# Causal mask of a half of the scores: one VectorE operation over both PSUM banks instead of one for each bank

## What is computed

```python
def _decay_mask(L):
    n = jnp.arange(L)
    nm = n[:, None] - n[None, :]
    g = jnp.asarray(GAMMAS)
    return jnp.where((nm >= 0)[None], g[:, None, None] ** jnp.maximum(nm, 0)[None], 0.0)

def _msr(X, WQ, WK, WV, WG, WO, gnw, gnb, D):
    Q = _xpos(jnp.einsum('bsh,nhd->bnsd', X, WQ), False)
    K = _xpos(jnp.einsum('bsh,nhd->bnsd', X, WK), True)
    V = jnp.einsum('bsh,nhd->bnsd', X, WV)
    A = jnp.einsum('bnsd,bntd->bnst', Q, K) * D[None]
    Y = jnp.einsum('bnst,bntd->bnsd', A, V)
    ...
    return G * jax.nn.sigmoid(G) * Yn @ WO
```

## Time and profile before

| | us |
|---|---|
| median of 3 runs | 2426.39 (2426.34 to 2426.5) |
| the profiled execution | 2424.55 |
| its span, first to last instruction | 2422.7 |
| busy: PE, DVE, POOL, ACT | 2223.8, 1869.4, 1762.4, 1550.3 |
| mean granted TensorE clock | 0.984 of full |

### The profile page before, as it was taken

One profiled execution on the slowest core, in us unless ns is written; L12 is line 12 of the kernel. 1 busy time (PEld: TensorE's weight loads), 2 busy tenths in 40 slices (PEclk: granted clock), 3 DMA queues, 4 the chain that ended last, 5 costly groups with the idle time before them and its releaser, 6 DMA issues.

```text
span 2422.7 us, 52427 instructions
## 1 busy us (share of the span) xinstructions
PE 2223.8 (92%) x18306; PEld 1940.9 (80%) x18306; DVE 1869.4 (77%) x5586; ACT 1550.3 (64%) x4986; POOL 1762.4 (73%) x1758
## 2 busy tenths in 40 slices
PE   0389999999999999999999999999999999996984
PEld 0268888888888888888888888888888888886874
DVE  6457888878787888888888888787888887867543
ACT  0156776776767777677677776767777677763442
POOL 4786777777777777777777777777777774334777
PEclk9989999999999999999999999999999999998997
DMA  2813131312122222213131313122221111002875
GB/s 98 311 40 101 25 112 29 111 29 96 44 72 67 72 69 71 72 29 111 27 112 27 110 30 113 28 72 66 72 69 36 34 28 36 1 30 79 254 229 158
DMA packets 110527, 192.17 MB, mean 79 GB/s; under 512 B 24388, under 2 KB 44998, under 8 KB 110160
## 3 DMA queue, kind: packets, MB, share of 16 engines
q1 hardware_dynamic: 66640, 97.96, 11.6%
q0 software_dynamic: 33280, 67.45, 9.9%
q10 hardware_dynamic: 10368, 23.67, 3.3%
HBM read 100.30 MB, written 89.73 MB: 78 GB/s over the span
## 4 chain that ended last, share of the span: by engine, by line
PE 74%; POOL 11%; DVE 5%; issue 5%; ACT 3%; DMA 2%; ACTq 1%; POOLq 0%; SPq 0%; DVEq 0%
PE psum L1211 64%; PE psum L1231 7%; POOL grams L621 4%; POOL gr L656 3%; PE psum L1282 3%; POOL out L683 2%; DVE hid L1058 2%; ACT qm L736 1%; DMA out<-h,e_id 1%; ACT qkT L734 1%; ACT xn L747 1%; POOL rstd L632 0%; DVE ms L1063 0%; DMA out<-side_n,e_id 0%; ACT hid L790 0%
## 5 line engine op out<-in xcount | busy, mean ns | idle before, releaser
L621 POOL DMA_INDIRECT grams<-gram_table,idx_all x768 | 780.4, 1016 | 193.6 <-issue 184.9
L1211 PE MATMUL psum<-xT,lw 128*128 128x256 f32 x1920 | 479.1, 383 | 0.2 <-ACT xT L722 0.2
L656 POOL TENSOR_TENSOR gr<-ms,con 128x8 f32<-128x8 f32 x192 | 325.9, 1697 | 154.7 <-DVE ms L1063 151.4
L1211 PE MATMUL psum<-lw,hid 128*128 128x129 f32 x3072 | 392.7, 277 | 1.9 <-ACT hid L766 1.9
L1211 PEld LDWEIGHTS psum<-lw,hid 128*128 128x128 f32 x3072 | 369.8, 192 | 15.0 <-issue 10.3
L1211 PEld LDWEIGHTS psum<-xT,lw 128*128 128x128 f32 x1920 | 339.1, 191 | 32.0 <-ACT xT L722 0.3
L632 POOL TENSOR_TENSOR rstd<-ss,con 128x2 f32<-128x2 f32 x320 | 232.1, 728 | 173.2 <-ACT squares L710 170.4
L766 ACT ACTIVATE hid<-psum,par 128x256 f32<-128x256 f32 x768 | 307.0, 482 | 10.8 <-PE psum L1211 7.9
L722 ACT ACTIVATE xT<-psum,par 128x256 f32<-128x256 f32 x384 | 214.8, 564 | 122.2 <-PE psum L1231 122.0
L1211 PE MATMUL psum<-lw,xT 128*128 128x256 f32 (+1 forms) x1536 | 287.6, 330 | 0.7 <-ACT xT L722 0.7
L1058 DVE TENSOR_TENSOR hid<-psum,con 128x512 f32<-128x512 f32 x384 | 249.0, 683 | 31.7 <-PE psum L1211 27.4
(11 more groups left out here) (200 smaller groups left out, 4689.1 us busy)
## 6 DMA issues: line engine op xcount, KB each, us to landing
routed_rows<-pad SPq DMA_DIRECT2D x265, 264.0 KB, 4.3
grams<-expert_w ACTq DMA_DIRECT2D x45, 321.0 KB
grams<-gram_table,idx_all POOLq DMA_INDIRECT x768
grams<-routed_rows SPq DMA_DIRECT2D x80, 132.0 KB
qm<-expert_w ACTq DMA_DIRECT2D x27, 321.0 KB
xb<-x SPq DMA_DIRECT2D x32, 256.0 KB, 3.5
lw<-layer_w SPq DMA_DIRECT2D x1, 2503.5 KB, 12.2
routed_rows<-row,slot POOLq DMA_INDIRECT x128, 2.4
```

What stands on the lines that cost most here:

```text
L621: pool.indirect_dma_start(grams[s][:, g, c, :], None, gram_table, bass.IndirectOffsetOnAxis(ap=idx_all[:, g, at:at + 1], axis=0))\
L656: pool.tensor_tensor(gr[s][:, c], ms[s][:, c], const("half")[:, 0:n], ALU.pow).then_inc(y_r[s], 1)
L1211: return pe.matmul(dst, lhsT, rhs, start=start, stop=stop)
```

## The change

For each half and layer, one DVE operation multiplies both banks at once: 1024 columns from two neighbouring banks, the mask broadcast over 2 x 4 blocks. It waits for bank b's signal, which is raised last, and raises `sc_s` by two. It takes the point in time that `mask0` had; `mask1`'s point is gone.

```diff
@@ -52,7 +52,6 @@
     "dve mask0": ((16.65, 14.05, 14.9), (16.67, 15.68, 10.8)),
-    "dve mask1": ((-1.7, -33.72, -32.34), (-36.06, -32.27, 11.41)),
     "dve ms": ((19.48, 19.3, 20.55), (21.98, 21.81, 20.47)),
@@ -1051,12 +1050,12 @@
-                for m in range(2):
-
-                    yield at(f"dve mask{m}", h, l)
-                    dve.wait_ge(sc_p[s], nth(k, 4, 2 * h + m))
-                    dve.tensor_tensor(A[s][:, h, m], chunks((a, b)[m]), causal.unsqueeze(1).to_broadcast([P, HEADS, P]),
-                                      ALU.mult).then_inc(sc_s[s], 1)
+                yield at("dve mask0", h, l)
+                dve.wait_ge(sc_p[s], nth(k, 4, 2 * h + 1))
+                dve.tensor_tensor(A[s][:, h, :],
+                                  psum[:, 4 * s + 2 * h:4 * s + 2 * h + 2, :].rearrange("p m (n q) -> p m n q", q=P),
+                                  causal.unsqueeze(1).unsqueeze(1).to_broadcast([P, 2, HEADS, P]),
+                                  ALU.mult).then_inc(sc_s[s], 2)
```

## The result

The changed kernel takes 2430.89 us (median of 20 runs, 2429.16 to 2433.54), the kernel before on the same chip 2426.35 us (20 runs, 2423.88 to 2427.16). The ratio is 1.0022, 95% interval 1.0016 to 1.0028: slower by 4.5 us between the medians. The interval lies clear of 1, but the size is about the 0.2% that the prediction took for the least that tells from no change. The predicted time was 2428.7 us.

The account below looks back on a forecast made before the run. TensorE bounds the kernel for most of the span, not VectorE's load. Chain gain -2.2, late z +4.3 and last pair of batches +0.2 make +2.3 us on 2426.4: 2428.7 us, forecast 2427.0 to 2430.7, range 2424.0 to 2432.0.

Parts of the forecast that it names:

- z late in stream 1: Half 1, layer 2: z ends 0.53 us later behind the merged mask; TensorE stands 0.29 us, 15 times, +4.3 us.
- a gain on the chain: Masks on the chain of work that ended last: merging saves 0.07 us per pair, -2.2 us together.
- rival A: At TensorE's zp weight load, z's lateness is covered after all; only the gain is left, 2424.2 us; chance 0.15.
- the merged operation: VectorE's mask over both banks: by width alone ends at 1.215 us and gives the engine on after 1.13 us.
- Rival B: Merged mask: reading two banks costs extra; as long as the pair it gives 2432.0 us, +0.23%; chance 0.13.
- the 5.0 us: Gain of the 32 masks on the chain by the skill page's formula, 157 ns less duration per merger.
- Both signals thus come at once, and this wait costs nothing here.: Merged mask's wait for the second bank's scores: the last two matmuls are in flight together, so no cost.
- Rival C: Second bank's scores come later; the 32 pairs lose 0.18 us each, sum +10 us, 2436.7 us; chance 0.03.
- 32 pairs, 0.07 us each: -2.2 us: Of 192 mask pairs, 32 lie on the chain; each merger gains 0.07 us there, and the gain arrives whole.
- the two chain places of a round: Per pair of batches: mask before the router's places matmul, and mask through router and GpSimd to scores; 0.07 us gain each.
- to spare: Stream 0's z: 0.65 us of cover against 0.53 + 0.05 us needed, so its lateness costs nothing, 0.07 us left.
- Rival D: VectorE is the hidden bound: all 192 gains on the path, -13.4 us, 2413.0 us; chance 0.02.

Follow-up runs that it names:

- pair_ahead_of_z: Kernel before, still two masks, but in 32 places the second mask stands directly behind the first, ahead of z: 2431.65 us against 2426.74 (1.0019).
- z_first: Changed kernel with the merged mask behind z instead of ahead in the 32 places, raise by two kept: 2427.15 us; kernel before 2426.22 (1.0004).
- pair_behind_z_stream1: Kernel before, still two masks, both behind z only in stream 1: 2426.02 us; kernel before 2425.82 (1.0000).
- wait_b: Kernel before, but the first mask too waits for the second bank's signal: 2427.99 us; kernel before 2426.74 (1.0008).
- one_signal: Changed kernel, mask raising by one, behind z only in stream 1, TensorE raising `sc_p` once per half: 2420.70 us; kernel before 2425.82 (0.9983).
- inc_one: Changed kernel, but the merged mask raises its semaphore by one and waiters count halves: 2427.96 us; kernel before 2426.22 (1.0006).
- inc_two: Kernel before, two masks in old order, each raising its semaphore by two, waiters asking for twice the number: 2429.27 us against 2426.74 (1.0008).
- behind_z_stream1: Changed kernel, merged mask raising by one and behind z only in stream 1: 2422.22 us; kernel before 2425.82 (0.9986).
- both: Changed kernel with the merged mask behind z in both streams and raising by one: 2423.27 us; kernel before 2426.22 (0.9989).

## Why the prediction was right or wrong

**Right: the sign, and the main term.** Two effects were set against each other, z late in stream 1 and a gain on the chain, with the loss the larger. The time lies in the stated range of 2424.0 to 2432.0 us, but 0.2 us above the band of 2427.0 to 2430.7 that the forecast itself was given. The order against z was shown alone (pair_ahead_of_z, +4.9 us) and taken back alone (z_first, -3.6; pair_behind_z_stream1, no change). Its size was 0.34 us at the place instead of 0.29, because z's second part took 0.53 us there and not 0.48. That rival A (z is covered) is out is seen in the load's wait of 0.32 us.

**Right: the merged operation.** 1225 ns against 1215, 1.13 us to the next start. (The 683 ns that the sum starts from is the mean; the median in the earlier trace rows is 681, which changes nothing.) Rival B, that two banks cost extra, is out. So are the 5.0 us that the prediction set beside its 2.2: the mask ended 0.06 us sooner than the pair, not 0.157.

**Wrong: "Both signals thus come at once, and this wait costs nothing here."** The matmuls do end together, as the earlier trace rows says, but the step from their ends to the signals was not looked at. The matmuls end 0.007 us apart, and by the semaphore events the raises take effect 0.043 us apart, in all traces with two of them. wait_b waits for the second alone: the mask shown starts 0.04 us later, the round is 0.10 us longer, and the time 1.25 us, with an interval that still includes no change. one_signal gets part of it back. Rival C had the right mechanism with the wrong origin and size.

**Missed: the raise by two.** The prediction gave `then_inc(sc_s[s], 2)` no term: it priced the instruction, not its wait. A waiting mask starts 0.07 us later for it. inc_one gets 2.8 us back; inc_two shows it without a merged mask.

Together they take 0.11 us from a gain of 0.06 at every waiting mask. The step "32 pairs, 0.07 us each: -2.2 us" thus became about +0.05 us at each of the two chain places of a round, and in stream 0 the mask's late start used up the 0.07 us that z had "to spare": its load came 0.04 to 0.05 us later.

**Too small: the number of places that gain.** The forecast let only the two chain places of a round gain, 0.14 us. Side by side with the kernel before, behind_z_stream1 and the changed kernel itself gain 0.06 us at three more places of a round, where the values or the step behind them wait for a mask for less than is listed as a wait. One is at 1083.25; weight loads of the kernel before, in order of time:

```profile
1082.89 0.19 PEld L1211 LDWEIGHTS psum<-lw,zp 128*128 128x128 f32 x1
1083.25 0.41 PEld L1211 LDWEIGHTS psum<-qkT,kv 128*128 128x128 f32 x3 [0.17 <-issue]
```

The mask that these values need ended at 1083.14 there (VectorE in order of time):

```profile
1081.86 1.28 DVE L1058 TENSOR_TENSOR hid<-psum,con 128x512 f32<-128x512 f32 x2
```

The idle time stands under "issue", not under the mask. Merging alone is worth 0.21 to 0.27 us a round.

**The balance of a round** of the changed kernel, by TensorE's starts beside the kernel before (medians over the rounds): +0.33 us at z in stream 1, +0.05 at each of the two chain places, +0.04 at z in stream 0, -0.06 at each of the three places. That makes 0.29 of the 0.36 us; the rest is small steps. That the forecast missed by only 2.2 us is partly luck: two costs that it lacked (0.21 us a round for the separate wait, 0.10 for the second signal) stood against gains that it lacked, here the three places.

**Rival D**, VectorE as the hidden bound: out. VectorE's busy time fell by 9.6 us (1869.4 to 1859.8) and the time rose.

What stays open is why z's second part takes 0.53 us instead of 0.48 in stream 1. The traces show what it goes with. All engines in order of time, in the changed kernel:

```profile
1026.30 1.02 POOL L620 DMA_INDIRECT grams<-gram_table,idx_all  x1 [0.19 <-issue]
...
1026.59 0.53 DVE L1067 SCALAR_TENSOR_TENSOR zp<-zp,par,sw 128x256 f32<-128x256 f32 x1
```

and in pair_ahead_of_z, where it takes 0.48:

```profile
1026.72 1.02 POOL L621 DMA_INDIRECT grams<-gram_table,idx_all  x1 [0.20 <-issue]
...
1027.08 0.48 DVE L1068 SCALAR_TENSOR_TENSOR zp<-zp,par,sw 128x256 f32<-128x256 f32 x1
```

In the changed kernel's trace 27 of the 192 take over 0.51 us. Each of them begins 0.29 to 0.30 us after GpSimd began a fetch of `grams`, or 0.07 to 0.09 us before it begins one, and no other does. So it is where z falls beside GpSimd's fetch that goes with the longer time, not the merged mask in front of it; in pair_ahead_of_z it falls 0.36 us behind. This was not tried apart.

## What to carry to other kernels

When operations are merged, price three things apart: the work itself, what now stands in front of what, and how the new instruction waits and signals. On an engine with a fixed order a merger takes away the place between the two halves, and what stood there comes later or earlier by a whole operation; ask which of the neighbours is ready and which has cover, stream by stream. Let a merged operation raise its semaphore by one and change what the waiters count, and let the engine that it waits for raise once.

## What the runs showed of the hardware

- **A VectorE instruction that raises a semaphore by two did not carry its wait as well here** (the changed kernel, z_first, inc_two). The wait becomes an instruction of the sequencer; if the engine has to wait, the work starts 0.09 us after the signal instead of 0.02. The Trainium skill (Trainium Kernel Development and Optimization, section Key Constraints) has compute semaphores go up by one. A raise by two kept the order here; its price is these 0.07 us. Where VectorE is busy with a longer operation when the signal comes, it costs nothing: behind z's second part (z_first) the mask starts 0.08 us before that one's end, as with a raise by one (both). Behind the short `ms` of 0.17 us it starts 0.01 us before its end instead of 0.08.
- **Two raises of one semaphore by matmuls that end 0.007 us apart take effect 0.043 us apart** (all traces but one_signal's), and a raise that nobody needs delays the one that is waited for: 0.050 us from the matmul's end to the raise's effect with two (behind_z_stream1), 0.024 with one (one_signal).
- A VectorE operation over two PSUM banks, 128x1024, takes 1225 ns, what the slope from 128x256 to 128x512 says to within 1%. Two of 128x512 give the next instruction its start after 1.20 us, the merged one after 1.14: each merger of two saves 0.06 us.
